# Preparing the feed-forward weights inside the attention stages instead of ahead of them

## The reference

```
n = layernorm(x)                         # over the 1024 features
for each of 16 heads of 64 features:
    c = n - mean over the 8192 tokens(n)
    out = softmax(c c^T) n
x = x + out
n = layernorm(x)
h = relu(q_5_10(q_4_3(n) q_4_3(w1)^T + q_4_3(b1)))    # w1 is 4096 x 1024
y = q_5_10(q_4_3(h) q_4_3(w2)^T + q_4_3(b2))          # w2 is 1024 x 4096
x = x + dropout(y)                       # fixed mask, scale 1.25
```

## Time and profile before

| what | value |
|---|---|
| median of 3 runs | 11030.04 us (11027.36 to 11040.63) |
| the profiled execution, its own time | 11021.43 us |
| its span, on the slowest core (core 3) | 11019.7 us |
| spans of the eight cores | 10995.9 to 11019.7 us |
| busy share of that span | DVE 52%, ACT 31%, PE 25%, PEld 7%, POOL 1% |
| first key tile's matmul of stage 0 starts | 3187.95 us |

### The profile page before, as it was taken

How to read it: one execution, slowest core, us unless ns; L and a number is a source line. 1 busy time by engine, 2 the same in 40 slices (tenths; PEclk the granted TensorE clock), 3 DMA queues, 4 the chain that set the end, 5 groups by cost and what they waited for, 6 DMA issues and landing times.

```text
span 11019.7 us, 63965 instructions; the slowest of 8 cores (10995.9 to 11019.7 us)
## 1 busy us (share of the span) xinstructions
PE 2751.0 (25%) x10512; PEld 748.6 (7%) x10512; DVE 5743.0 (52%) x8314; ACT 3388.4 (31%) x5265; POOL 100.4 (1%) x209
## 2 busy tenths in 40 slices
PE   0000000000026633432442343244224333421112
PEld 0000000000001100100110010011001000100001
DVE  7677774777600045355435534543554454357775
ACT  0011110111038834533541353344135434510000
POOL 0000000000000000000000000000000000000000
PEclk9999999999999966776775677677567767755556
DMA  4620002000022111110121011012101101210001
GB/s 117 142 64 23 23 23 81 23 23 23 24 75 48 41 29 22 27 36 21 26 48 32 22 27 36 21 25 49 32 21 27 37 21 25 46 26 10 11 17 37
DMA packets 1004845, 402.77 MB, mean 37 GB/s; under 512 B 961456, under 2 KB 965552, under 8 KB 996272
## 3 DMA queue, kind: packets, MB, share of 16 engines
q1 hardware_dynamic: 988208, 323.18, 13.0%
q0 software_dynamic: 16256, 75.51, 1.8%
HBM read 289.46 MB, written 75.50 MB: 33 GB/s over the span
## 4 chain that ended last, share of the span: by engine, by line
DVE 50%; ACT 23%; issue 10%; PE 8%; DMA 7%; DVEq 2%; ACTq 0%; SPq 0%; POOLq 0%; POOL 0%
ACT etA L573 9%; ACT etB L576 7%; DVE attnN L160 6%; DVE qb L160 5%; DVE qa L160 4%; DVE attnN L159 4%; DVE qd L159 3%; PE ndA L593 2%; PE megaA L561 2%; DVE qe L159 2%; DMA out_fm<-ych 2%; DVEq L133 2%; PE ndB L597 1%; DMA w1qn<-hq 1%; DVE Drec L621 1%
## 5 line engine op out<-in xcount | busy, mean ns | idle before, releaser
L561 PE MATMUL megaA<-qfq,kch 64*128 64x512 bf16 x2048 | 815.3, 401 | 3240.7 <-DMA kch<-Kfm 3240.7
L573 ACT ACTIVATE etA<-megaA,cpool 128x512 bf16<-128x512 f32 x2048 | 1410.2, 689 | 494.6 <-PE megaB L566 441.8
L621 DVE RECIPROCAL Drec<-Dall 1x512 f32<-1x512 f32 x32 | 106.9, 3341 | 2728.1 <-ACT Dall L616 2728.1
L576 ACT ACTIVATE etB<-megaB,cpool 128x512 bf16<-128x512 f32 x2048 | 1398.3, 683 | 0.0
L593 PE MATMUL ndA<-etA,vsl 128*65 128x512 bf16 x2048 | 796.2, 389 | 2390.4 <-DVE qc L237 1036.0
L566 PE MATMUL megaB<-qfq,kch 64*128 64x512 bf16 x2048 | 815.4, 401 | 0.0
L597 PE MATMUL ndB<-etB,vsl 128*65 128x512 bf16 x2048 | 797.7, 390 | 0.0
L450 PE MATMUL ffnps<-xq,w1t 128*128 128x512 bf16 x896 | 352.0, 559 | 1619.7 <-DVE qa L213 1393.7
L160 DVE SCALAR_TENSOR_TENSOR attnN<-attnN 128x1024 f32<-128x1024 f32 x576 | 705.7, 1225 | 60.6 <-DVE attnN L159 0.9
L218 ACT ACTIVATE qb<-qa 128x512 f32<-128x512 f32 x128 | 80.7, 631 | 1924.3 <-DVE qa L213 1924.3
L160 DVE SCALAR_TENSOR_TENSOR qb<-qd,qb 128x512 f32<-128x512 f32 (+1 forms) x806 | 554.9, 688 | 86.5 <-DVE qd L159 3.2
(11 more groups left out here) (144 smaller groups left out, 4685.7 us busy)
## 6 DMA issues: line engine op xcount, KB each, us to landing
kch<-Kfm SPq DMA_DIRECT2D x32, 2048.0 KB, 8.3
vsl<-Xn SPq DMA_DIRECT2D x2048, 32.0 KB, 1.8
xbuf<-x_tok SPq DMA_DIRECT2D x64, 512.0 KB, 3.9
w1t<-w1qT SPq DMA_DIRECT2D x128, 256.0 KB, 2.9
w2t<-w2qT SPq DMA_DIRECT2D x32, 1024.0 KB, 8.5
Xn<-xnc POOLq DMA_DIRECT2D x64, 256.0 KB, 4.0
Kfm<-kch POOLq DMA_DIRECT2D x8, 2048.0 KB, 8.8
attnR<-w SPq DMA_DIRECT2D x16, 512.0 KB, 3.8
```

The source lines that it names most:

```text
L561: e.matmul(t["megaA"][kpar], t["kch"][par][0:64, kt * 128:(kt + 1) * 128], t["qf"][0:64, p * SW:(p + 1) * SW], start=True, stop=True, tile ...
L573: self.op("scalar", "act", lambda e, kpar=kpar: e.activation(t["etA"][kpar], t["megaA"][kpar], AF.Exp, bias=cp[:, 3:4], scale=1.0))
L576: self.op("scalar", "act", lambda e, kpar=kpar: e.activation(t["etB"][kpar], t["megaB"][kpar], AF.Exp, bias=cp[:, 3:4], scale=1.0))
L621: self.vop(lambda e, h0=h0: e.reciprocal(t["Drec"][h0], t["Dall"][h0]))
```

## The change

`w_prep` is gone. The weight work is cut into 128 units in a list, `prep_q`. A unit `wj` takes a 128 x 1024 piece of a weight: load into one of two new buffers `wbN`, two calls of `q43_tile` on 128 x 512 each with the buffers `qa` to `qd`, output into one of the two `xnc` buffers, store by POOL. A unit `wtr` is one DMA transpose of 1024 x 128 into one of two new staging buffers `stg`, and its store by POOL. The list is eight times "8 `wj`, then 8 `wtr` of what they made": four quarters of `w1`, then four of `w2`. `pump_prep` emits the next units of the list at the end of each slot: 10 in each slot of stage 0 and, after the five feed-forward units, 8 in each slot of stage 1 until the list is empty. The buffers `wbN` and `stg` take the place of `ident` (with its load), `onesbf` and one of the four `vsl` buffers. Feed-forward units wait on SP for the stores of `w1qT` or `w2qT`. The diff, without renamed and removed declarations:

```diff
-        id_ld = self.dma("sync", t["ident"], t["identin"], sem="l_id")
...
-        for par in range(4):
+        for par in range(3):
...
-        def w_prep(wsrc, nat, dst, nrow_tiles, ncols, stage, stage_sem):
-            if cfg.NCH * SW >= 4096:
-                WQ = 1024
-                wbufs = (t["attnN"][:, 0:WQ], t["attnN"][:, WQ:2 * WQ],
-                         t["attnN"][:, 2 * WQ:3 * WQ], t["attnN"][:, 3 * WQ:4 * WQ])
-            else:
-                WQ = SW
-                wbufs = None
-            for j in range(nrow_tiles):
-                par = j % 2
-                wb = t["wbuf"][par][:, 0:ncols]
-                self.wait("sync", "dve", self.wbuf_done[par])
-                ldv = self.dma("sync", wb, wsrc[j * 128:(j + 1) * 128, :],
+        ntr1 = max(1, cfg.NHJ * 128 // 1024)
+        nwtr1 = (cfg.D // 128) * ntr1
+        nwtr2 = cfg.HF // 128
+        nwtr = nwtr1 + nwtr2
+        self.w1T = [16 * ((nwtr1 + 1) // 2), 16 * (nwtr1 // 2)]
+        self.w2T = [16 * ((nwtr + 1) // 2), 16 * (nwtr // 2)]
+
+        def emit_prep_unit(u):
+            if u[0] == "wj":
+                _, src, nat, row0, col0, ncol, last = u
+                par = self.prep_par
+                self.prep_par ^= 1
+                wb = t["wbN"][par][:, 0:ncol]
+                self.wait("sync", "dve", self.wbN_done[par])
+                ldv = self.dma("sync", wb,
+                               src[row0:row0 + 128, col0:col0 + ncol],
                                sem=f"l_wb{par}")
                 self.wait("vector", f"l_wb{par}", ldv)
                 self.wait("scalar", f"l_wb{par}", ldv)
-                self.wait("vector", "s_tr0", self.tr_store[0])
-                for sl in range(ncols // WQ):
-                    self.q43_tile(wb[:, sl * WQ:(sl + 1) * WQ],
-                                  t["wq"][:, sl * WQ:(sl + 1) * WQ], WQ, 3,
-                                  bufs=wbufs)
-                self.wbuf_done[par] = self.cnt["dve"]
-                self.wait("gpsimd", "dve", self.wbuf_done[par])
-                self.wait("gpsimd", "s_tr0", self.tr_store[0])
-                self.tr_store[0] = self.dma(
-                    "gpsimd", nat[j * 128:(j + 1) * 128, :],
-                    t["wq"][:, 0:ncols], sem="s_tr0")
-            nat_done = self.cnt["s_tr0"]
-            for ch in range(ncols // 128):
-                self.wait("sync", "s_tr0", nat_done)
-                self.wait("sync", "s_tr1", self.tr_store[1])
+                self.wait("vector", f"s_nat{par}", self.nat_mark[par])
+                self.wait("vector", f"s_vt{par}", self.vt_store[par])
+                for sl in range(ncol // SW):
+                    self.q43_tile(wb[:, sl * SW:(sl + 1) * SW],
+                                  t["xnc"][par][:, sl * SW:(sl + 1) * SW],
+                                  SW, 3)
+                self.wbN_done[par] = self.cnt["dve"]
+                self.wait("gpsimd", "dve", self.wbN_done[par])
+                self.nat_mark[par] = self.dma(
+                    "gpsimd", nat[row0:row0 + 128, col0:col0 + ncol],
+                    t["xnc"][par][:, 0:ncol], sem=f"s_nat{par}")
+                self.wj_marks[last] = (self.cnt["s_nat0"], self.cnt["s_nat1"])
+            else:
+                _, nat, dst, ch, r0, nrow, dep = u
+                spar = self.prep_spar
+                self.prep_spar ^= 1
+                g = self.wj_marks[dep]
+                self.wait("sync", "s_nat0", g[0])
+                self.wait("sync", "s_nat1", g[1])
+                self.wait("sync", f"s_dst{spar}", self.stg_store[spar])
                 if self.on("sync"):
                     self.eng.dma_start_transpose(
-                        stage[:, 0:nrow_tiles * 128],
-                        nat[:, ch * 128:(ch + 1) * 128]
-                    ).then_inc(self.sems[stage_sem], 16)
-                sld = self.bump(stage_sem, 16)
-                self.wait("gpsimd", stage_sem, sld)
-                self.tr_store[1] = self.dma(
-                    "gpsimd", dst[ch * 128:(ch + 1) * 128, :],
-                    stage[:, 0:nrow_tiles * 128], sem="s_tr1")
-
-        w_prep(t["w1"], t["w1qn"], t["w1qT"], cfg.NHJ, cfg.D,
-               t["w2t"][0], "l_w20")
-        w_prep(t["w2"], t["w2qn"], t["w2qT"], cfg.NCH, cfg.HF,
-               t["w1t"][0], "l_w10")
-        p2_tr = [self.cnt["s_tr0"], self.cnt["s_tr1"]]
-        self.wait("vector", "s_tr0", p2_tr[0])
-        self.wait("vector", "s_tr1", p2_tr[1])
+                        t["stg"][spar][:, 0:nrow],
+                        nat[r0:r0 + nrow, ch * 128:(ch + 1) * 128]
+                    ).then_inc(self.sems[f"l_tr{spar}"], 16)
+                trl = self.bump(f"l_tr{spar}", 16)
+                self.wait("gpsimd", f"l_tr{spar}", trl)
+                self.stg_store[spar] = self.dma(
+                    "gpsimd", dst[ch * 128:(ch + 1) * 128, r0:r0 + nrow],
+                    t["stg"][spar][:, 0:nrow], sem=f"s_dst{spar}")
+
+        prep_q = []
+        wid = 0
+        for qq in range(ntr1):
+            for j in range(8 * qq, min(8 * qq + 8, cfg.NHJ)):
+                prep_q.append(("wj", t["w1"], t["w1qn"], j * 128, 0, cfg.D,
+                               wid))
+                wid += 1
+            for ch in range(cfg.D // 128):
+                prep_q.append(("wtr", t["w1qn"], t["w1qT"], ch, qq * 1024,
+                               min(1024, cfg.NHJ * 128), wid - 1))
+        nq2 = cfg.HF // cfg.D
+        for q in range(nq2):
+            for j in range(cfg.NCH):
+                prep_q.append(("wj", t["w2"], t["w2qn"], j * 128, q * cfg.D,
+                               cfg.D, wid))
+                wid += 1
+            for ch in range(8 * q, 8 * q + 8):
+                prep_q.append(("wtr", t["w2qn"], t["w2qT"], ch, 0, cfg.D,
+                               wid - 1))
+        self.prep_q = prep_q
+        self.prep_i = 0
+
+        def pump_prep(kmax):
+            n = 0
+            while self.prep_i < len(self.prep_q) and n < kmax:
+                emit_prep_unit(self.prep_q[self.prep_i])
+                self.prep_i += 1
+                n += 1
...
                 self.wait("sync", "pe", self.w1t_free[mpar])
+                self.wait("sync", "s_dst0", self.w1T[0])
+                self.wait("sync", "s_dst1", self.w1T[1])
...
                 self.wait("sync", "pe", self.w2t_free[mpar])
+                self.wait("sync", "s_dst0", self.w2T[0])
+                self.wait("sync", "s_dst1", self.w2T[1])
...
-                self.wait("sync", "s_tr0", p2_tr[0])
-                self.wait("sync", "s_tr1", p2_tr[1])
...
-                            vpar = kt % 4
+                            vpar = kt % 3
...
                     if s > 0:
                         for u in units[p * per_slot:(p + 1) * per_slot]:
                             emit_ffn_unit(s - 1, u[0], u[1])
+                    pump_prep(10 if s == 0 else 8)
             else:
+                pump_prep(len(self.prep_q))
                 for u in units:
                     emit_ffn_unit(s - 1, u[0], u[1])
...
-        t["wq"] = t["hq"][:, 0:HF]
+        t["wbN"] = [sb(f"wbN{i}", [128, D], F32) for i in range(2)]
+        t["stg"] = [sb(f"stg{i}", [128, 1024], BF16) for i in range(2)]
```

More of the change, by code:

```diff
@@ L94, in __init__ @@
         self.kch_free = [0, 0]
-        self.vsl_free = [0, 0, 0, 0]
+        self.vsl_free = [0, 0, 0]
         self.mega_freeA = [0, 0]
@@ L122, in __init__ @@
         self.hq_ready = 0
+        self.prep_par = 0
+        self.prep_spar = 0
+        self.wbN_done = [0, 0]
+        self.nat_mark = [0, 0]
+        self.stg_store = [0, 0]
+        self.wj_marks = {}
+        self.w1T = [0, 0]
+        self.w2T = [0, 0]
     def on(self, name):
@@ L305, in emit @@
                 t["vsl"][par][:, 129:130], 1.0))
-        self.op("gpsimd", "gp", lambda e: e.memset(t["onesbf"], 1.0))
         self.op("gpsimd", "gp", lambda e: e.memset(t["onesf32"], 1.0))
@@ L311, in emit @@
             self.wait(en, "gp", gp_init)
-        self.wait("tensor", "l_id", id_ld)
         for tt in range(cfg.NTT):
@@ L773, in build_program @@
         t["cpool"] = sb("cpool", [128, len(CPOOL_VALS)], F32)
-        t["ident"] = sb("ident", [128, 128], BF16)
-        t["onesbf"] = sb("onesbf", [1, 128], BF16)
         t["onesf32"] = sb("onesf32", [128, 1], F32)
@@ L794, in build_program @@
         vslh = [es.enter_context(nc.sbuf_tensor(f"vsl{i}", [128, 130], BF16))
-                for i in range(4)]
+                for i in range(3)]
         t["vsl"] = [h[:] for h in vslh]
@@ L827, in build_program @@
         t["resid"] = [t["attnR"], t["sqch"]]
[L828 to L831, removed]
         t["megaA"] = [es.enter_context(nc.psum_tensor(f"megaA{i}", [128, SW], F32))[:]
@@ L849, in build_program @@
                          f"l_w1{i}", f"l_w2{i}", f"s_vt{i}", f"s_tr{i}",
-                         f"s_kc{i}", f"l_vs{i + 2}"]
+                         f"s_kc{i}", f"l_tr{i}", f"s_dst{i}", f"s_nat{i}",
```

(1 more changed line is left out.)

## The result

| | median | runs | against before |
|---|---|---|---|
| before | 11026.57 us | 8 | |
| changed | 11200.26 us | 8 | 1.0157, 95% interval 1.0146 to 1.0168 |

A forecast was written before the change was run, and what follows sets the result against it. Bound: up to 3188 us PE idles, mostly for weight preparation; moved, it stays serial through ACT's queue. -2570 + 2684 + 37 + 8 + 2 = +161 us, median 11190 us; range 11120 to 11310, 8 in 10 within 11140 to 11265.

The forecast's parts named there:

- The moved work is not hidden: Slots' ends: ACT's queue puts each quantizer call before the next pair's exponentials, so its length counts in full.
- Removed, -2570: Start of attention: it needs only `Kfm`, so the first exponential comes at 618.3 instead of 3188.66, -2570 us.
- The calls, +2684: Weight quantizer: 128 calls on 512 columns at 20.97 us each, +2684 us, 550 of it only the narrower tile.
- Stage 0's ends, +37: Stage 0's slot ends: 7 for later starts, -46 for covered ends, +64 and +11 around transposes, in sum +37 us.
- Stage 1, +8: Slots p0, p2, p4 of stage 1: ACT waits out the feed-forward tail, +2.7 us each, +8 us.
- three value buffers, +2: Key loops of all four stages: a few loads late with one buffer fewer, 0 to 12 us, taken as 2.
- The total: Whole kernel: +161 us on the profiled execution's 11021.4, forecast for the median 11190 us, 1.5% slower, chance 0.78.
- The upper bound of 11310: Whole kernel: top of the range 11120 to 11310 us, with all error bounds of calls, transposes and key loads at once.
- The tie: Whole kernel: within 22 us of 11030, needing 139 us of terms wrong in one direction; chance 0.03.
- The single-buffer pace: Slots' ends in stage 0: each transpose takes the full 6.2 us despite two buffers, +75 us, 11265 us; chance 0.14.
- Rival 2: Quantizer calls: the narrow tile has no extra price, so the sum falls by 550 to 10640 us; chance 0.03.
- Rival 3: Key loops: DVE quantizes during them, the move doesn't serialize, up to 700 us hidden, 10490 us; chance 0.02.

The follow-up runs named there:

- Run 9: Against a base with 512-column calls at slots' ends, six value buffers, transposes mostly in key loops: 56 of 128 calls spread over key loops; 10231.23 us, 0.9274 of before.
- Run 1: The kernel before with one number changed, quantizer calls on 512 columns instead of 1024 in the old place: 11596.89 us, ratio 1.0513 to before.
- run 2: The changed kernel with its quantizer calls on 1024 columns instead of 512: 10603.72 us, ratio 0.9613 to the kernel before.
- run 4: The kernel before with three value buffers instead of four, nothing else: 11037.97 us, ratio 1.0006 to before.
- run 7: The changed kernel with one staging buffer for all transposes instead of two in turn: 11294.37 us, ratio 1.0235 to the kernel before.
- run 3: The changed kernel with transposes inside the next slot's key loop, one every seven key tiles, instead of at slots' ends: 11170.21 us, ratio 1.0129 to before.
- run 5: The changed kernel with transposes inside key loops, one every seven key tiles, and six value buffers instead of three: 11137.73 us, ratio 1.0098 to before.
- run 6: The changed kernel with six value buffers and transposes in key loops from key tile 20, one every five: 11061.82 us, ratio 1.0028 to before.

## Why the prediction was right

- *The moved work is not hidden.* Right. No exponential runs between the ACT operations of a call, and slot p0 of stage 0 is 354 us longer, of 352 forecast. (DVE's count rose by 1728 as forecast, to 10042, and its busy time by 277 us.) Run 9 shows that their place in ACT's queue is the reason: the same calls, with their ACT operations spread out, cost a quarter.
- *Removed, -2570.* Measured -2577 on core 3. The last store of `Kfm` was issued at 590.69 and landed 6.6 us later (assumed: 596.13 and 8.8), and the first exponential came 14.7 us after that, not 13.3. These 7 us are chance: on core 1, the slowest, the first exponential is at 620.09.
- *The calls, +2684, of which 550 for the narrow tile.* Measured 20.96 us a call. Run 1 gives the narrow tile 568 us and run 2 takes the change from 1.0157 to 0.9613 with it undone. This term decides the sign.
- *Stage 0's ends, +37.* Mechanism right, size off: +71. By slots, over the calls, forecast and measured: p0 16 and 19, p1 -8 and -1, p2 29 and 35, p3 -10 and -9, p4 -2 and 9, p5 22 and 27, p6 -10 and -9, p7 0 and 1. The term that was too small is the pace of transposes. I took the old cycle of 6.2 us, measured beside nothing else, for two; six took SP 18.98 us at p2, and eight 28.83 us at p4, where I had 14.7 and 20.9. The transposes land later than before, 3.6 us in the median (3.9 on average) against 3.2. And the exponential comes 11.5 us after the key load's issue at p2 (1617.11 to 1628.58), not 9.6.

```profile
2134.87 28.83 SPq L427 DMA_TRANSPOSE stg<-w1qn  x8
...
2164.10 0.82 SPq L146 DMA_DIRECT2D wbN<-w  x2
```

- *Stage 1, +8; three value buffers, +2.* Measured +9 and +4; run 4 bounds the buffers at 0.15% of the time.
- *The total.* It is closer than its terms, and that is luck: +34 in stage 0's ends stand against -7 at the start and -13 in the tail, both on core 3. The upper bound of 11310 was also added up wrong: 42 and 75 and three times 5 on 11190 are 11322. Nothing hangs on it. The tie would have needed 139 us of errors in one direction.
- *Rivals.* The single-buffer pace costs 94 us (run 7), a little above its 75, and did not happen, though stage 0's ends took 34 us more than forecast. Rival 2 is refuted by runs 1 and 2. Rival 3 names a real chance, but not one that this change takes: it needs the reordering of run 9.
- *Not forecast:* the stretch after the last copy is 13 us shorter on core 3, and 8 to 18 us on every core. Its code is unchanged. DVE's waits for the output store are 11 us of the 18 on core 1, the page's core now. The two rows are of the line that waits, before (the same on cores 1 and 3) and changed (core 1). On core 3 the changed kernel has 74.3 us, 8 of its 13:

```profile
  DMA out_fm<-ych: 81.9, 11
```

```profile
  DMA out_fm<-ych: 71.0, 11
```

Why those stores land sooner stays open. The granted clock of TensorE is 0.67 on average now and was 0.79 before. A stretch without matmuls shows 1.00, and the changed kernel hardly has one after 612 us. The loops show no price for it: 32 of them took 4 us more in sum, and a score matmul (`megaA`) takes 401 ns on the page of either kernel.

## What to carry to other kernels

Work moved next to idle engines is hidden only if every in-order queue that it touches lets the other work pass: here ACT's, then SP's, then POOL's. Read the order of each queue at the place before counting on the idle time in the profile. When a move shrinks the scratch space, price the narrower tile first: it cost 568 us, where the whole change lost 174.

## What the runs showed of the hardware that I had not expected

A second staging buffer gives 1.6 to 1.9 times the rate of transposes of 1024 x 128 and their stores, and not twice. Between the first two and the last, two buffers took 4.1 us a transpose at p2, (18.98 - 2.5) / 4, 4.4 at p4, (28.83 - 2.5) / 6, and 3.4 to 3.9 in the other groups of eight. One buffer (run 7, core 3) took 6.6 us at p2, (34.02 - 1.15) / 5, 7.1 at p4, (51.06 - 1.15) / 7, and 6.1 to 6.4 in the others. So the pace that I took from the quiet stretch before, 6.2 for one, was already too good for p2 and p4.

Value loads of 32 KB in flight beside a transpose land in 2.2 us in the median instead of 1.8, and in up to 4.1 (run 3). Three buffers are too few for that and six are enough (runs 3, 5 and 6).
